# x and the identity in one transfer, and the first transposed rows copied by two engines

## The reference, cut to what matters

```python
x = x + _L0_xattn_ref(_layernorm(x, axis=-1), ctx_512, ...)
x = x + _L0_attn_ref(_layernorm(x, axis=-1), ...)
x = x + _L0_ffn_ref(_layernorm(x, axis=-1), ...)
x = x + _L1_xattn_ref(_layernorm(x, axis=-1), ctx_512, ...)
x = x + _L1_attn_ref(_layernorm(x, axis=-1), ...)
x = x + _L1_ffn_ref(_layernorm(x, axis=-1), ...)
```

```python
m = jnp.mean(x, axis=axis, keepdims=True)
v = jnp.var(x, axis=axis, keepdims=True)
return (x - m) / jnp.sqrt(v + eps)
...
q_hk = (hidden_q @ Wq.T).reshape(b, s, H, K)
```

## Time and profile before

| | us |
|---|---|
| median of 3 runs | 345.86 |
| lowest and highest | 345.24, 345.91 |
| the profiled execution | 345.36 |
| its span, first to last instruction | 343.6 |

### The profile page before, as it was taken

The page is one execution under the profiler, slowest core; times in us unless marked ns, Lnnn a source line. Parts: engine busy times, 40 slices in busy tenths (PEclk is TensorE's granted clock), DMA queues, the critical chain, the costliest instruction groups (busy, mean ns, idle before and its releaser), DMA issues.

```text
span 343.6 us, 5417 instructions
## 1 busy us (share of the span) xinstructions
PE 332.1 (97%) x2195; PEld 220.0 (64%) x2197; DVE 153.4 (45%) x337; ACT 104.7 (30%) x229; POOL 37.3 (11%) x76
## 2 busy tenths in 40 slices
PE   7999999999999999989999999999999999999997
PEld 6888889999988566754444343434356756644465
DVE  2049667777772135744303212212348455753221
ACT  1102225666765002433222123231112175220110
POOL 1012000000000020042000000000028420002110
PEclk9999999999999999999999999999999999999999
DMA  7999999950002500025699999999989940000000
GB/s 263 420 423 446 424 388 440 418 229 2 0 2 78 229 0 2 0 78 230 253 401 365 365 420 360 358 433 361 441 340 423 426 195 1 2 0 0 0 0 32
DMA packets 7944, 79.44 MB, mean 231 GB/s; under 512 B 1008, under 2 KB 1904, under 8 KB 3056
## 3 DMA queue, kind: packets, MB, share of 16 engines
q1 hardware_dynamic: 7920, 79.09, 56.6%
HBM read 78.83 MB, written 0.26 MB: 230 GB/s over the span
## 4 chain that ended last, share of the span: by engine, by line
PE 85%; DMA 6%; DVE 4%; SPq 2%; issue 1%; POOL 1%; ACT 1%; DVEq 0%; POOLq 0%
PE ps L1572 12%; PE ps L1748 9%; PE ps L1302 8%; PE ps L1276 8%; DMA ra<-in_wq 6%; PE ps L1600 5%; PE ps L1619 4%; PE ps L1380 4%; PE ps L1555 3%; PE ps L1670 3%; PE ps L1611 2%; PE ps L1431 2%; PE ps L1190 2%; PE ps L1451 2%; PE ps L1193 2%; PE ps L1774 2%
## 5 line engine op out<-in xcount | busy, mean ns | idle before, releaser
L1572 PE MATMUL ps<-rd,ra 128*64 128x384 f32 x256 | 44.4, 489 | 0.1
L1276 PE MATMUL ps<-rd 128*128 128x128 f32 x256 | 35.9, 276 | 0.1
L1572 PEld LDWEIGHTS ps<-rd,ra 128*64 128x64 f32 x256 | 18.0, 137 | 26.5 <-issue 25.6
L1276 PEld LDWEIGHTS ps<-rd 128*128 128x128 f32 x256 | 32.8, 195 | 0.4 <-DVE rd L789 0.2
L996 DVE SCALAR_TENSOR_TENSOR ra<-ra,ps 128x192 f32<-128x192 f32 x16 | 5.7, 354 | 58.8 <-ACT ra L634 58.8
L1302 PE MATMUL ps<-rd,ra 128*128 128x129 f32 x256 | 31.2, 274 | 0.0
L1302 PEld LDWEIGHTS ps<-rd,ra 128*128 128x128 f32 x256 | 29.8, 191 | 0.0
L634 ACT ACTIVATE ra<-ps 128x192 f32<-128x192 f32 x16 | 5.3, 330 | 63.5 <-PE ps L1572 63.5
L1748 PE MATMUL ps<-rd,xnT 128*128 128x512 f32 x56 | 24.5, 594 | 0.0
L817 DVE TENSOR_REDUCE xn<-ps 128x128 f32<-128x512 f32 x32 | 21.7, 681 | 0.7 <-PE ps L1276 0.7
L412 POOL TENSOR_SCALAR sv<-sv 128x1 f32<-128x1 f32 x6 | 1.5, 247 | 183.5 <-DVE sv L735 129.8
(11 more groups left out here) (306 smaller groups left out, 515.3 us busy)
## 6 DMA issues: line engine op xcount, KB each, us to landing
rd<-in_ring SPq DMA_DIRECT2D x8, 2560.0 KB, 8.9
rd<-in_ring SPq DMA_DIRECT2D x8, 2048.0 KB, 8.4
rd<-in_f1gu SPq DMA_DIRECT2D x8, 1024.0 KB, 13.4
ra<-in_e SPq DMA_DIRECT2D x2, 2562.0 KB, 14.1
rb<-in_b SPq DMA_DIRECT2D x1, 5122.0 KB, 21.7
rb<-in_wb SPq DMA_DIRECT2D x1, 5120.0 KB, 31.9
ra<-in_wr SPq DMA_DIRECT2D x4, 1152.0 KB, 17.4
ra<-in_wq SPq DMA_DIRECT2D x3, 1024.0 KB, 14.6
```

Of the source, the lines that this page charges most:

```text
L1276: ins = pe.matmul(ps[:, 2 * (u % 2) + j // 4, P * (j % 4):P * (j % 4) + P], kvT[:, u % 2, P * j:P * j + P], rows, start=True, stop=True)
L1572: ins = pe.matmul(ps[CAP * e:CAP * e + CAP, 2 + p % 2, 0:2 * I0].rearrange("p (g n) -> p g n", g=2), moe_xq[q % 2][:, c, CAP * e4:CAP * e4 ...
```

## The change

The identity leaves `cst` and becomes columns 513 to 640 of the tile and of the input of x; one transfer brings both, 2,564 bytes for each partition. `cst` keeps the other constants in 332 columns and is loaded whole where its second part was loaded. The transposes of the first layer norm go to two banks, 7 and 5. VectorE copies blocks 0 and 1 from bank 7, and ScalarE blocks 2 and 3 from bank 5, ahead of its first `query_copy`. TensorE waits for both before `queries(0)`. As `xTa_ready` counts one copy more, its later thresholds rise by one. The idle products behind the transposes become 5 instead of 7. TensorE waits for `ld_x` where it waited for `ld_const`.

```diff
-K_ID, K_MASK, K_U, K_IOTA, K_M16, K_M32, K_N = 0, 128, 192, 320, 448, 456, 460
+K_MASK, K_U, K_IOTA, K_M16, K_M32, K_N = 0, 64, 192, 320, 328, 332
...
-        x = sb("x", [P, D + 1])
+        x = sb("x", [P, D + 1 + P])
...
-        ident = cst[:, K_ID:K_ID + P]
+        ident = x[:, D + 1:D + 1 + P]
...
-            sp.dma_start(x[:, 0:D], x_in).then_inc(ld_x, 16)
-            sp.dma_start(cst[:, 0:P], consts_d[:, 0:P]).then_inc(ld_const, 16)
+            sp.dma_start(x[:, :], x_in).then_inc(ld_x, 16)
...
-            sp.dma_start(cst[:, P:K_N], consts_d[:, P:K_N]).then_inc(ld_c64, 16)
+            sp.dma_start(cst[:, :], consts_d).then_inc(ld_c64, 16)
...
+            act.wait_ge(xT_ps, 1)
+            act.activation(xnT[:, 2:4, :].rearrange("p c t -> p (c t)"), ps[:, 5, 0:256], ACT.Copy).then_inc(xTa_ready, 1)
             for g in range(GROUPS):
                 query_copy(g)
...
-                dve.tensor_copy(xnT[:, :, :].rearrange("p c t -> p (c t)"), ps[:, 7, :]).then_inc(xT_ready, 1)
+                dve.tensor_copy(xnT[:, 0:2, :].rearrange("p c t -> p (c t)"), ps[:, 7, 0:256]).then_inc(xT_ready, 1)
...
-                        ins = pe.transpose(ps[:, 7, c * P:(c + 1) * P], src[:, c, :], ident)
+                        ins = pe.transpose(ps[:, 7 - 2 * (c // 2), c % 2 * P:(c % 2 + 1) * P], src[:, c, :], ident)
                     ins.then_inc(xT_ps, 1)
-                    keep_clock(7)
+                    keep_clock(5)
...
-                pe.wait_ge(xTa_ready, i)
+                pe.wait_ge(xTa_ready, i + 1)
...
                     pe.wait_ge(xT_ready, 1)
+                    pe.wait_ge(xTa_ready, 1)
...
-            pe.wait_ge(ld_const, 16)
+            pe.wait_ge(ld_x, 16)
...
-                pe.wait_ge(xTa_ready, nxt)
+                pe.wait_ge(xTa_ready, nxt + 1)
...
-            pe.wait_ge(xTa_ready, 5)
+            pe.wait_ge(xTa_ready, 6)
...
-    c[:, K_ID:K_ID + P] = np.eye(P)
...
-        "x": v["x"].reshape(P, D), "consts": cst, "rope": rope,
+        "x": np.concatenate([v["x"].reshape(P, D), np.zeros((P, 1), np.float32), np.eye(P, dtype=np.float32)], axis=1), "consts": cst, "rope": rope,
```

More of the change, by code:

```diff
@@ L263, in build @@
         g_rstd = sb("g_rstd", [P, 16])
-        ld_x, ld_const, ld_ctx, ld_kr, ld_b0, ld_c64 = map(sem, ("ld_x", "ld_const", "ld_ctx", "ld_kr", "ld_b0", "ld_c64"))
+        ld_x, ld_ctx, ld_kr, ld_b0, ld_c64 = map(sem, ("ld_x", "ld_ctx", "ld_kr", "ld_b0", "ld_c64"))
         ld_r = [sem(f"ld_r{g}") for g in range(GROUPS)]
```

## The result

The changed kernel takes 344.80 us (median of 20 runs, 344.33 to 345.42); the kernel before, run beside it, 345.45 us (20 runs, 344.66 to 347.03). The ratio is 0.998, with a 95% interval of 0.9972 to 0.9988: faster by 0.65 us, between 0.41 and 0.97 us. The forecast was -0.20 us, with a chance of 0.82 that the two kernels differ by less than 0.2%. The profiled execution took 344.37 us with a span of 342.6 us, 1.0 us less than before's span.

A forecast was written before the change was run, and what follows sets the result against it. The landing of the fourth query weights at 26.9 us was taken to set the end. Only the dropped issue counted, -0.20 us, other terms 0: 345.86 - 0.20 = 345.66, say 345.7 us, range 344.8 to 346.3 us.

The forecast's parts named there:

- What bounds the kernel: Start: the fourth query weights' landing at 26.89 us moves the end equally; earlier TensorE work is covered by 1.66 us of waits.
- The term of the issue that goes: SyncE's load stream: without the identity's own transfer, query weights fill idle DMA engines from 2.10 to 2.56 us; -0.20 us.
- The upper bound: Load stream: if landings depended on issue times alone, they would come 0.48 us earlier, the fast end of the term.
- the rival in which the slow beginning is made good: Load stream, 1.6 to 3.6 us: the pair of small transfers causes all the loss; -0.84 us, 345.0 us, chance 0.08.
- The estimate from the Trainium skill's table: Identity's 64 KB transfer: alone 0.95 us, at the larger one's pace 0.38 us, so merging saves 0.57 us; not used.
- x lands 0.2 us later: Start: x's 66 KB more delay its landing and `bn_stats`, rstd, xn up to the transposes by 0.24 us.
- The copy: Behind the transposes: VectorE's 0.69 us copy becomes 0.424 us there and 0.383 us on ScalarE, side by side; -0.27 us.
- Start of the queries: TensorE, 7.59 us before: +0.24 - 0.27 + 0.05 = +0.02 us, under 1.66 us of waits, so 0 us at the end.
- The three DMA waits still there: Sign of being right: TensorE still waits for the rank weights (0.51 us), `wkr` (0.47 us) and fourth query weights (0.68 us).
- The identity's place: Slower rival: 206 products reading the identity inside x's tile each take 50 ns more; 10.3 us, 356.0 us, chance 0.04.
- The clock: TensorE before the transposes: idle grows from 0.71 to about 0.95 us without bringing back the slow pace; charged nothing.

The follow-up runs named there:

- a1: Changed kernel with the first half of the first query weights issued by ScalarE at about 0.7 us, beside SyncE's x; 344.72 us, ratio 0.9981.
- the merge alone: Changed kernel with x and identity in one transfer, but the single 128x512 copy and 7 idle products as before the change; 344.85 us, ratio 0.9971.
- the holds: Changed kernel, SyncE held behind x without added transfer; first weights issued at 1.31, 1.66, 2.16, 2.66 us: 344.73, 345.72, 345.20, 346.68 us.
- hold of half a microsecond: Changed kernel with SyncE held behind x by GpSimd memsets, no transfer added, first query weights issued at 1.66 us; 345.72 us, ratio 1.0009.
- i1late: Changed kernel with an added 64-byte transfer, read by nobody, issued behind both halves of the first query weights; 344.73 us, ratio 0.9967.
- i1: Changed kernel with one tiny issue, a 64-byte transfer nobody reads, in the identity's place between x and the first weights; 345.48 us, ratio 0.9992.
- d10: Changed kernel with SyncE held behind x, no transfer added, first query weights issued at 2.16 us; 345.20 us, ratio 0.9993.
- s1: Changed kernel with an added 64 KB transfer in 128 rows of 512 bytes, read by nobody, in the identity's place; 345.42 us, ratio 0.9996.
- d15: Changed kernel with SyncE held behind x, no transfer added, first query weights issued at 2.66 us; 346.68 us, ratio 1.003.
- a3: Changed kernel with ScalarE issuing the first half of the first query weights once GpSimd's ones are written, near 1.0 us; 344.36 us, ratio 0.9961.
- c1: Kernel before with only the two banks, two copies and 5 idle products; identity keeps its own transfer; 345.67 us, ratio 1.001.

## Why the prediction was wrong

*What bounds the kernel* held. The end follows the start of the products on the fourth weights one for one in all profiles, and that start is their landing plus 0.04 to 0.05 us, except in a1 and in the two profiles with a fallen clock (below). The split copy and `keep_clock` cost and gained nothing, and x's later landing stayed under the waits, as the sum said.

*The term of the issue that goes was the step that failed.* It took -0.20 us from the idle share between 2.10 and 2.56 us in the earlier trace rows. Measured is -0.65 us (of the 0.86 us between the forecast 345.66 us and 344.80 us, the other 0.41 us is the kernel before, which took 345.45 us beside it and 345.86 us earlier), -0.82 us for the same kernel in another group, and -0.74 us for the merge alone in a third. The place was right, as the holds show, but the price was read in one window of 0.46 us, as though all that a break costs lay where the engines are seen idle. Most of it comes later: the stream has moved less by 7.6 us (217 to 245 GB/s against 249 to 266), and the mean of the engines lands 0.53 us later on average. A wider gap between the mean and the last engine (1.62 us against 1.30 us on average) may add to it, within a wide scatter.

*The upper bound was wrong too.* That with "the issue times alone" the landings "would come 0.48 us earlier" was used as the end of the range and as the argument against the rival in which the slow beginning is made good (-0.84 us, chance 0.08). The merge brings the weights 0.48 us forward, and all three medians are beyond that; the interval of the merge alone (ratio 0.9971, 0.9958 to 0.9983) begins at 0.59 us. The hold of half a microsecond took back 0.85 to 1.0 us by the medians, from 0.65 or 0.82 us under the kernel before to 0.20 us over it, though the interval of its ratio (0.9989 to 1.0029) leaves room for 0.5 us. That rival's price, the whole loss between 1.6 and 3.6 us, was near the three medians. Its cause, as the prediction put it, was not: the holds pay it with no transfer, and i1late has a small transfer and doesn't pay. The estimate from the Trainium skill's table (DMA: Bandwidth & Descriptors, Measured), 0.57 us, came out nearer than the forecast's 0.20 us. But that table is for transfers issued from GpSimd, and its rule, a cost per small transfer, isn't what the runs show; an issue of 64 bytes or none at all costs about the same, and only ahead of the first weights.

*x lands 0.2 us later*: `bn_stats` at 3.59 us, forecast near 3.6 us. The 0.24 us between x and the identity came from two rounded times; the landings in the trace are 3.37 and 3.54 us, 0.17 us apart. *The copy*: 0.42 and 0.39 us side by side, as expected. *Start of the queries*: forecast 7.61 us, 7.49 us measured. *"The three DMA waits still there"*: wrong for the rank weights, which landed at 15.53 us, 1.4 us earlier.

*The identity's place* (slower): its products (here those from 30 us on) take what they took in the earlier trace rows, so that rival is out:

```profile
L1234 PE MATMUL ps<-x,rd x14: 271/272/328, 29.8 to 36.5; 128*128 128x128 f32 x14
L1295 PE MATMUL ps<-x,sv x16: 322/322/323, 37.7 to 101.5; 128*128 128x128 f32 x16
```

*The clock.* Nothing was lost there, but the pause that was forecast, 0.95 us ahead of the transposes, didn't come in this profile. The 27 idle products took 5.50 us instead of 4.40 us, TensorE was still on them when xn was written, and the transposes followed at 6.31 us without a wait. In the profile of the merge alone TensorE did idle there, for 0.76 us, and the seven products behind it took 273 ns each, with the granted clock at 1.00:

```profile
6.22 0.63 PE L1150 MATMUL ps<-x,xn 128*128 128x128 f32 x4 [0.76 <-DVE xn L762]
6.68 0.93 PE L1143 MATMUL ps<-ones 128*128 128x256 bf16 x7
```

That the clock is safe doesn't hold in general, see below.

## What to carry to other kernels

Where a kernel's start waits for a stream of loads, find the load whose landing ends the last such wait; what happens on the engines before it is free up to the sum of the waits, and a break in the stream's first microseconds can cost as much as it lasts, or more. Put the first large load right behind the one that the engines need first, and small loads behind it; a second issuing engine can start the stream earlier still, as long as the urgent load has a head start. Don't price a break in a stream by the idle share of one short window: hold the queue in an experiment, and read the median and several landings, because two profiles of one kernel differed by 0.66 us in the landing here, and by 1.07 us with one tiny issue.

## What the runs showed of the hardware that was not expected

*A late landing can cost the clock as well.* In the first i1 profile TensorE waited 1.51 us for the rank weights. TensorE's timeline, and then windows with the granted clock ahead of the DMA share:

```profile
17.86 0.88 PE L1208 MATMUL ps<-ra 128*64 128x128 f32 x12 [1.51 <-DMA ra<-in_wr]
19.23 0.93 PE L1252 MATMUL ps<-rd 64*128 64x128 f32 x8 [0.49 <-DMA rd<-in_wkr]
20.08 1.55 PE L1208 MATMUL ps<-ra 128*64 128x128 f32 x12
...
28.54 3.74 PE L1224 MATMUL ps<-xnT,ra 128*128 128x128 f32 x32
```

```profile
18.00:20.00 2.00, 1.51 (x20) 1.16 (x18) 0.00 (x0) 0.00 (x0) 0.00 (x0) 0.90 1.00 422
20.00:22.00 2.00, 2.00 (x16) 1.59 (x15) 1.02 (x2) 0.00 (x0) 0.00 (x0) 0.50 1.00 414
22.00:24.00 2.00, 2.00 (x17) 1.76 (x16) 0.67 (x3) 0.00 (x0) 0.00 (x0) 0.75 1.05 432
```

The granted clock is 0.50 (1.2 GHz) from 20 to 22 us, twelve products take 1.55 us instead of 0.88 us, and TensorE reaches the fourth group at 28.54 us, 0.7 us after its weights landed (27.83 us). This execution took 346.87 us, 1.4 us over the kernel's median, to which its late landing adds as well. The profile of d10 has the same after a wait of 1.09 us; s1 and d15, with waits of 1.62 and 1.13 us, kept 1.00.

*One packet of instructions seems to hold one DMA engine up.* In every profile one packet of 16,384 bytes on the instruction queue starts between 14.6 and 16.6 us and runs for about 1.0 us. In a3, whose engines are otherwise close together, the landings are (us):

```
transfer           first   15th of 16   last
rank weights 1     14.03   14.49        14.58
wkr                15.32   15.84        17.09
query weights 4    24.05   24.57        25.82
```

The packet starts at 15.04 us. From then on one engine is 1.25 us behind the other 15, and still so when the fourth weights land; the landing that ends the wait is this engine's. Which engine a packet used isn't recorded, so this is read from the times and was not tested by moving the packet. Other profiles show the same step: with one tiny issue, with s1 and with the holds to 2.16 and 2.66 us, the last engine is 0.6 to 1.0 us behind the mean in the first rank weights and 2.0 to 2.3 us behind in the second. These are the four profiles with a q4 of 28 us or more. In others, as c1 and the merge alone, the last engine's distance hardly changes. It would fit if it mattered whether the held-up engine was ahead or behind, and it can explain a part of why landings of one kernel differ. Of the 0.66 us between the two profiles of the changed kernel (25.88 and 26.54 us) it is the smaller part: 0.39 us lie in the mean of the engines.
